# Self attention on one core: slots taken two at a time, all jobs at full tile shape, projections as three products of rounded parts, GpSimd splitting the maxima

## What is computed

```python
def _L1_ffn_ref(x, Wq, Wkv, Ws, Wo, bo):
    s = jax.nn.sigmoid(x @ Ws)
    vals, idx = jax.lax.top_k(s, TOPK)
    scores = jnp.zeros_like(s).at[bi, ti, idx].set(vals)
    q = (x @ Wq).reshape(b, t, H, DH).transpose(0, 2, 1, 3)
    kv = (x @ Wkv).reshape(b, t, 2, H, DH).transpose(2, 0, 3, 1, 4)
    k, v = (kv[0], kv[1])
    attn = jax.nn.softmax(jnp.einsum('bhid,bhjd->bhij', q * scale, k), axis=-1)
    out = jnp.einsum('bhij,bhjd->bhid', attn, v)
    proj = jnp.einsum('bhtd,hde->bhte', out, Wo) + bo[None, :, None, :]
    return jnp.einsum('bhte,bth->bte', proj, scores)
```

## Time and profile before

| | |
|---|---|
| time, median of 3 runs | 2458.72 us (2457.88 to 2459.5) |
| the profiled execution's own time | 2457.71 us |
| its span, first to last instruction | 2455.7 us |
| PE, share of the span | 85% |
| DVE, ACT, POOL | 60%, 37%, 36% |
| TensorE's granted clock, mean | 0.923 of full speed |
| `self_gates`, first to last instruction | about 1487 to 1559 us |
| `self_attention`, until PE's loop starts | about 1559 to 1625 us |
| one batch of the loop (four units) | 100.05 us |

### The profile page before, as it was taken

How to read it: one execution, slowest core, us unless ns; L and a number is a source line. 1 busy time by engine, 2 the same in 40 slices (tenths; PEclk the granted TensorE clock), 3 DMA queues, 4 the chain that set the end, 5 groups by cost and what they waited for, 6 DMA issues and landing times. The chain is left out here.

```text
span 2455.7 us, 38024 instructions
## 1 busy us (share of the span) xinstructions
PE 2085.7 (85%) x11977; PEld 1378.2 (56%) x11977; DVE 1471.1 (60%) x2334; ACT 918.0 (37%) x1568; POOL 884.1 (36%) x801
## 2 busy tenths in 40 slices
PE   5760499999999972799999997389999999999997
PEld 2660499999999970333333337145555455555454
DVE  7840244554555443799998875356575666656655
ACT  4520133333333420366666662122232332323332
POOL 0057723551555013455453330113333333333322
PEclk9955799999999985799999995699999999999998
DMA  6572233323332234244443333233232322323231
GB/s 226 203 295 103 79 119 125 113 79 130 118 120 68 78 96 123 77 127 131 126 125 113 111 108 131 58 83 74 61 91 65 86 61 61 94 63 84 65 77 49
DMA packets 155315, 257.46 MB, mean 105 GB/s; under 512 B 25414, under 2 KB 74606, under 8 KB 151914
## 3 DMA queue, kind: packets, MB, share of 16 engines
q1 hardware_dynamic: 111778, 176.24, 25.0%
q0 software_dynamic: 15328, 44.61, 5.5%
q10 hardware_dynamic: 28160, 35.99, 4.5%
HBM read 124.81 MB, written 75.43 MB: 82 GB/s over the span
## 5 line engine op out<-in xcount | busy, mean ns | idle before, releaser
L1207 DVE TENSOR_REDUCE ca_negmax<-ca_na 128x2 f32<-128x1024 f32 x272 | 330.8, 1220 | 42.1 <-PE ca_na L935 39.7
L1057 ACT ACTIVATE ca_pr<-ca_st 128x512 f32<-128x512 f32 x512 | 279.3, 599 | 131.8 <-PE ca_st L949 130.2
L680 DVE TENSOR_TENSOR ex_h<-ex_up,ex_sg 128x512 f32<-128x512 f32 x136 | 94.0, 692 | 306.0 <-ACT ex_sg L643 198.7
L1839 DVE TENSOR_REDUCE sa_negmax<-sa_na 128x1 f32<-128x512 f32 x272 | 182.7, 674 | 132.5 <-PE sa_na L1659 127.9
L935 PE MATMUL ca_na<-ca_k_stack,ca_q_stack 64*128 64x512 f32 x544 | 212.0, 467 | 23.8 <-DVE ca_negmax L1207 21.0
L603 PE MATMUL ex_gp<-ex_xp,moe_gu_p 128*128 128x256 f32 x1632 | 222.2, 286 | 1.6 <-DVE ex_xp L666 1.4
L949 PE MATMUL ca_st<-ca_q_stack,ca_k_stack 64*128 64x512 f32 x512 | 205.7, 462 | 18.0 <-ACT ca_pr L1057 17.4
L616 PE MATMUL ex_yp<-moe_dn_p,ex_hp 128*128 128x256 f32 x1632 | 209.3, 286 | 11.9 <-DVE ex_hp L670 11.9
L603 PE MATMUL ex_up<-ex_xp,moe_gu_p 128*128 128x256 f32 x1632 | 218.1, 283 | 0.0
L1827 POOL TENSOR_TENSOR sa_acc<-sa_acc,sa_pr 128x1024 f32<-128x1024 f32 x64 | 151.6, 2368 | 170.2 <-ACT sa_pr L1778 170.2
L1823 POOL TENSOR_TENSOR sa_acc<-sa_pr 128x1024 f32<-128x1024 f32 x32 | 75.2, 2349 | 381.6 <-ACT sa_pr L1778 381.6
(11 more groups left out here) (284 smaller groups left out, 3786.4 us busy)
## 6 DMA issues: line engine op xcount, KB each, us to landing
sa_q<-sa_qh SPq DMA_DIRECT2D x140, 128.0 KB
sa_k<-sa_kh SPq DMA_DIRECT2D x140, 128.0 KB
ex_raw_m<-masks ACTq DMA_DIRECT2D x34, 512.0 KB, 3.7
moe_gu_raw<-gateupT POOLq DMA_DIRECT2D x8, 2048.0 KB, 8.3
ca_k_stack<-cross_k SPq DMA_DIRECT2D x216, 64.0 KB
ca_q_stack<-cross_q SPq DMA_DIRECT2D x216, 64.0 KB
expert_rows<-rt_zeros SPq DMA_DIRECT2D x20, 512.0 KB, 15.4
cross_q<-ca_qp SPq DMA_DIRECT2D x10, 1024.0 KB, 5.1
```

The costliest lines, as they stand in the source:

```text
L1057: act.activation(pr[:, s // HG % 2, s % HG, :], st[s % 2][:, :], ACT.Exp, scale=DK ** -0.5).then_inc(exp_done, 1)
L1207: dve.tensor_reduce(negmax[:, g % 2, 1 - r % 2, :, r // 2], na[r % 2][:, :, :], AX.X, ALU.max, negate=True).then_inc(max_done, 1)
L1839: dve.tensor_reduce(negmax[:, par, h, t:t + 1], na[s % 2][:, :], AX.X, ALU.max, negate=True).then_inc(max_done, 1)
```

## The change

The changed kernel computes the same. It differs in these points.

- The loop over 8 slots becomes a loop over 4 rounds of two slots. A round is: both `score_b`, a place for jobs, both `score_a`, a place for jobs, `values`, a place for jobs. So there are 12 places for jobs in a unit.
- q, k and v are computed from rounded parts: x and the weights are split in `self_gates` (ACT copies the rounded part, POOL subtracts), and each product is the three terms of the list `TERMS`, so 6 rounded matmuls for q and 6 for k. v is made for two pairs of heads and two token tiles at a time (12 rounded matmuls of 256 columns), in units 0 (two), 2 and 3 (one each). x goes through HBM in both parts, 1 MB for a batch instead of 512 KB.
- The maxima are split by POOL instead of DVE, at the start of the unit that uses them. The stationary side is a full 128 columns, mostly zero, and the product is rounded.
- Gates and bias are matmuls over all 128 partitions (the unused ones are zero), with the bias in three terms too.

```diff
 def self_gates(nc, io, x, mv, rstd, ident, iota8, xT_d, gT_d, weights, wo, bo3):
+            def low(b):
+                pool.wait_ge(xh_ready, b + 1)
+                pool.tensor_tensor(xp[:, b % 2, 1, :, :], xt[:, :, b * S:(b + 1) * S], xp[:, b % 2, 0, :, :].bitcast(F32), ALU.subtract).then_inc(xl_ready, 1)
+            for b in range(2):
+                low(b)
+            for i, n in enumerate(weights):
+                pool.wait_ge(wh_ready, i + 1)
+                pool.tensor_tensor(weights[n][:, 1, :, :], raw[n][:, :, :], weights[n][:, 0, :, :].bitcast(F32), ALU.subtract).then_inc(wl_ready, 1)
+                low(b + 1 + i)
...
-                sp.wait_ge(xt_ready, (b + 1) * TB)
-                sp.dma_start(xT_d.rearrange("(c p) n -> p c n", p=P)[:, :, b * S:(b + 1) * S], xt[:, :, b * S:(b + 1) * S]).then_inc(stored, 16)
+                sp.wait_ge(xl_ready, b + 1)
+                sp.dma_start(xT_d.rearrange("(r c p) n -> p r c n", r=2, p=P)[:, :, :, b * S:(b + 1) * S], xp[:, b % 2, :, :, :].bitcast(F32)).then_inc(x_put[b % 2], 16)
...
             def copy_out(t):
+                if t % TB == TB - 1:
+                    b = t // TB
+                    act.wait_ge(xt_ready, t + 1)
+                    if b >= 2:
+                        act.wait_ge(x_put[b % 2], 16 * (b // 2))
+                    act.copy(xp[:, b % 2, 0, :, :], xt[:, :, b * S:(b + 1) * S]).then_inc(xh_ready, 1)
+                    if b == 1:
+                        act.wait_ge(w_in, 16 * 5)
+                        for n in weights:
+                            act.copy(weights[n][:, 0, :, :], raw[n][:, :, :]).then_inc(wh_ready, 1)
 def self_attention
+        sel2 = m.sb("sel2", [P, SH * H], F32R)
+        gparts = m.sb("gparts", [P, S], F32R)
+        xT = m.sb("xT", [P, 2, KC, S], F32R)
+        parts = m.sb("parts", [P, 2, 2, TB, P], F32R)
...
+            JOBS += {0: [("q", 0, 0), ("k", 0, 2), ("v2a", 0, 4), ("sum", 0, 5), ("v2b", 0, 6), ("m0", 0, 7), ("m1", 0, 9), ("gate", 0, 10)],
+                     1: [("q", 1, 0), ("k", 1, 2), ("o0", 1, 4), ("sum", 1, 5), ("o1", 1, 6), ("m0", 1, 7), ("m1", 1, 9), ("gate", 1, 10)],
+                     2: [("q", 2, 0), ("k", 2, 2), ("v0a", 2, 4), ("sum", 2, 5), ("m0", 2, 6), ("m1", 2, 7), ("gate", 2, 9)],
+                     3: [("q", 3, 0), ("k", 3, 2), ("v0b", 3, 4), ("sum", 3, 5), ("m0", 3, 6), ("m1", 3, 7), ("gate", 3, 9)]}[g]
+        FIRST = ["q", "k"] * 3 + ["v0a", "v0b", "m0", "m1"]
+        TERMS = ((0, 0), (0, 1), (1, 0))
...
-                        sp.wait_ge(misc_full, job(b, g, "v") + 1)
+                        sp.wait_ge(misc_full, job(b, g, "v2b") + 1)
                         load_x(after)
...
+                    for i in range(KC):
+                        for wr, xr in TERMS:
+                            last = pe.matmul(misc[:, :], w[:, wr, i, c * P:(c + 1) * P], xT[:, xr, i, :],
+                                             start=(i == 0 and (wr, xr) == TERMS[0]), stop=(i == KC - 1 and (wr, xr) == TERMS[-1]))
...
+                    for r in range(TB):
+                        for s in (2 * r, 2 * r + 1):
+                            score_b(g, s, u)
+                        jobs(g, 3 * r, b)
+                        for s in (2 * r, 2 * r + 1):
+                            score_a((g + 2) % C, b if g < 2 else b + 1, s, u + 2)
+                        jobs(g, 3 * r + 1, b)
+                        if r == 0:
...
+                            values((g - 1) % C, TB - 1)
...
+                            values(g, t)
+                        jobs(g, 3 * r + 2, b)
...
+            pool.memset(parts[:, :, :, :, :].bitcast(F32), 0.0).then_inc(set_up, 1)
+            def split_max(a, par, h):
+                pool.wait_ge(max_done, a * SLOTS + (h * TB + TB + 2))
+                pool.tensor_tensor(parts[:, par, h, :, H], negmax[:, par, h, :], ones[:, 0:TB], ALU.mult).then_inc(mh_ready, 1)
+                pool.wait_ge(mh_ready, a * 2 + (h + 1))
+                pool.tensor_tensor(parts[:, par, h, :, H + 1], negmax[:, par, h, :], parts[:, par, h, :, H].bitcast(F32), ALU.subtract).then_inc(ml_ready, 1)
...
                 for g in range(C):
                     u = b * C + g
+                    for h in range(2):
+                        split_max(u + 1, (g + 1) % 2, h)
                     pool.wait_ge(misc_full, job(b, g, "sum") + 1)
...
+                if h == 0 and t == 0 and not (isinstance(a, int) and a < 2):
+                    dve.wait_ge(ml_ready, a * 2 - 2)
...
-                if t == TB - 1:
-                    dve.wait_ge(max_done, a * SLOTS + (s + 3))
-                    dve.tensor_copy(parts[:, par, h, :, 0].bitcast(F32R), negmax[:, par, h, :]).then_inc(mh_ready, 1)
-                    dve.wait_ge(mh_ready, a * 2 + (h + 1))
-                    dve.tensor_tensor(parts[:, par, h, :, 1].bitcast(F32R), negmax[:, par, h, :], parts[:, par, h, :, 0], ALU.subtract).then_inc(ml_ready, 1)
```

More of the change, by code:

```diff
@@ L1611, in project @@
                     if name == "q":
                         pe.wait_ge(xT_in, b * 16 + 16)
-                if name == "v":
-                    for t in range(piece * TB // count, (piece + 1) * TB // count):
-                        for i in range(KC):
-                            last = pe.matmul(misc[:, t * P:(t + 1) * P], xT[:, i, t * P:(t + 1) * P], wv[:, i, c * P:(c + 1) * P],
-                                             start=(i == 0), stop=(i == KC - 1))
-                else:
-                    w = wq if name == "q" else wk
-                    for i in range(piece * KC // count, (piece + 1) * KC // count):
-                        last = pe.matmul(misc[:, :], w[:, i, c * P:(c + 1) * P], xT[:, i, :], start=(i == 0), stop=(i == KC - 1))
@@ L1622, in project @@
-                if piece == count - 1:
-                    last.then_inc(misc_full, 1)
+                    w = weights["sWq" if name == "q" else "sWk"]
+                    for i in range(KC):
+                        for wr, xr in TERMS:
+                            last = pe.matmul(misc[:, :], w[:, wr, i, c * P:(c + 1) * P], xT[:, xr, i, :],
+                                             start=(i == 0 and (wr, xr) == TERMS[0]), stop=(i == KC - 1 and (wr, xr) == TERMS[-1]))
+                last.then_inc(misc_full, 1)
@@ L1690, in _, with jobs @@
                         max_rows(nf - 2 + h, 0, 0, h)
+            def jobs(g, p, b):
+                u = b * C + g
+                for name in jobs_at(g, p):
+                    n = job(b, g, name)
+                    if name[0] == "m":
+                        max_rows(n, u + 1, (g + 1) % 2, int(name[1]))
+                    elif name == "sum":
+                        sums(n, u)
+                    elif name == "gate":
+                        if g == 1:
+                            pe.wait_ge(gT_in, b * 32 + 32)
+                        gates(n, (g - 1) % C)
+                    elif name[0] == "o":
+                        output(n, b, int(name[1]))
+                    else:
+                        project(n, name, (g + 3) % C, b if g == 0 else b + 1)
             with pe.Fori(0, B) as b:
@@ L1727, in _ @@
             for i in range(2):
-                output(last_job(f"o{i}"), B, i, (0, 1))
+                output(last_job(f"o{i}"), B, i)
         @block.scalar
@@ L1768, in _, with jobs @@
             act.activation(tock[:, :], ident[:, 0:1], ACT.Exp)
+            def jobs(g, p, b):
+                for name in jobs_at(g, p):
+                    n = job(b, g, name)
+                    if name == "sum":
+                        sum_out(n, b * C + g)
+                    elif name in "qk":
+                        head(n, name, None, (stack_in[(g + 2) % C], b * LOAD + (2 * LOAD if g >= 2 else LOAD)))
+                    elif name[0] == "v":
+                        v_out(n, name)
+                    elif name[0] == "m":
+                        m_out(n, (g + 1) % C, int(name[1]))
             with act.Fori(0, B) as b:
@@ L1891, in _, with jobs @@
                     maximum(a, s, a)
+            def jobs(g, p, b):
+                u = b * C + g
+                for name in jobs_at(g, p):
+                    n = job(b, g, name)
+                    if name in "qk":
+                        rest(n, name, u * 2 + (6 + "qk".index(name)))
+                    elif name == "gate":
+                        gate(n, u)
+                    elif name[0] == "o":
+                        add(n, int(name[1]), (b + (B - 1)) % B)
             with dve.Fori(0, B) as b:
```

200 lines of the change are left out of this document (91 added, 109 removed).

## The result

The changed kernel takes 2332.89 us, median of 4 runs (2331.47 to 2333.42), where the kernel before takes 2458.3 (2455.19 to 2459.5, 4 runs). The ratio is 0.9491, 95% interval 0.9474 to 0.9507, so 125 us went. The forecast was 2334. Its profiled execution took 2333.27 us, its span is 2331.0.

The account below looks back on a forecast made before the run. The prediction took PE to bound the loop, busy 96.1 of a batch's 100.05 us. It saved 16.6 us a batch, 133 in eight, and added 8 in `self_gates`: -125, so 2334 us (2316 to 2350).

Parts of the forecast that it names:

- E: Rival: gaps on PE drop the loop's clock to 1.2 GHz for part of each batch, slower than before; 2%.
- q, k and v: Loop, PE: rounded matmuls save 2.4 us a batch for q and k, 1.8 for v.
- Maxima: Loop, PE: a maxima job falls from 1.14 to 0.48 us, saving 5.3 us a batch over eight jobs.
- A: Rival: rounded 128-column matmuls cost 0.235 us, so maxima save 1.6 instead of 5.3; total 2363 us; 14%.
- Gate: Loop, PE: at full depth each of four gates saves 0.385 us, 1.5 a batch.
- Bias: Loop, PE: the bias falls from 0.845 to 0.12 us, four jobs saving 2.9 us a batch.
- Sums: Loop, PE: sums right behind `values` in the same tile shape save 4 x 0.35 = 1.4 us a batch.
- Old and new waits: Loop, PE, per batch: 4.0 us of waits go; 1.9 come behind ACT's exponential, 0.8 from missed handovers.
- `self_gates` +8: Block before the loop: ACT copies +3.5, last copy +1, POOL memset +1.8, POOL holding DVE +2; in all +8 us.
- C: Rival: POOL's 11 subtractions hold DVE fully in `self_gates`, +24 us on the +2 taken; total 2358; 8%.
- Start and end of `self_attention`: Outside the loop's batches: changes of a few us both ways, taken as 0, bounds -3 and +3.
- D: Rival: neither the wait behind the exponential nor missed handovers come, -2.7 us a batch; total 2313; 5%.

Follow-up runs that it names:

- experiment 7: Changed kernel with scores and jobs ordered slot by slot, plus the old fp32 two-column maxima matmul: 2348.38 us; or plus short gate and bias matmuls: 2331.57 us.
- experiment 4: Changed kernel with job m1 at place 8, behind `values`, in all units: 2317.09 us.
- experiment 8: Changed kernel with ACT's copies and POOL's subtractions of the weights moved behind the sigmoid in `self_gates`: 2332.57 us.
- experiment 10: Changed kernel without POOL's subtractions of x, its low part set to zero once: 2336.08 us, a single run.
- experiment 6: Changed kernel with the maxima split by DVE again and POOL's four operations gone: 2339.31 us.
- experiment 9: Changed kernel with the slot-by-slot order and the weights' copies and subtractions behind the sigmoid: 2307.72 us.

## Why the prediction was right, and where its steps were not

- **What bounds the loop.** Right. PE's work and its waits fill a batch before and after, at a clock of 1.00, so E never came near. Eight batches gave 126.5 of the 124.7 us.
- **q, k and v.** Right in sum: 4.2 forecast, 4.1 when undone. q and k were worth more (2.9 for 2.4) and v less (1.2 for 1.8). The 1.885 us of v before start right behind `values` and hold part of what leaving their tile shape costs, which the 1.205 of `values` had counted already (after the change k takes 1.49 behind `values`, q 1.37 behind scores).
- **Maxima.** Right to a tenth in size: 5.3 forecast, 4.8 measured with no wait about (experiment 7). The forecast priced all eight jobs like m0, which stands between scores. m1 stood right behind `values` in the kernel before:

```profile
1919.94 0.39 PE L1659 MATMUL sa_na<-sa_k,sa_q 128*128 128x512 f32 x1
1920.26 1.08 PE L1675 MATMUL sa_av<-sa_pr,sa_vw 128*64 128x512 f32 x4
1921.27 1.03 PE L1604 MATMUL sa_misc<-all_ident,sa_parts 128*2 128x128 f32 x8
...
1922.57 0.40 PE L1668 MATMUL sa_st<-sa_q,sa_k 128*128 128x512 f32 x1
```

  `values` and m1 together take 1922.57 - 1919.94 less two paces, 2.16, where 1.205 + 1.14 would be 2.345, so m1 cost 0.96 and not 1.14, 0.74 less in a batch. The reason given failed too: "the eight records are short and the rest is entering and leaving a tile two columns wide". Between scores the fp32 product costs 0.80 - 0.39 = 0.41 of it and the two columns 0.25; before `values`, which change the tile shape themselves, the columns cost nothing. The bound from 256 columns held: four rounded matmuls of 128 columns take 0.39 to 0.44 us, so A fell. The Trainium skill's figure ("TensorE: Matmul & The Clock Gate", section "Back-to-back issue gap"), 81 ns for each, would have made 0.32; the trace has about 0.11, for this rounded type.
- **Gate.** Right: 0.385 forecast, 0.38 measured between scores. Where the gate stands before `values` now, in units 0 and 1, undoing it costs 0.17 or, behind a wait, nothing.
- **Bias.** Half an output job takes 1.84 us where it took 2.55, 0.71 saved for 0.725 forecast. I laid it to "the bias and its 8-row tile"; the depth is 0.29 of it, the rest fp32.
- **Sums.** Right: `values` and sums take 2.06 together, counted as before, against twice 1.205: 0.35 saved in a unit, as forecast. No run undoes this term alone.
- **Old and new waits.** The 4.0 went, the new one is 0.4 to 0.5 us in each unit for the reason given (experiment 4 removes it by a place). Of the 0.8 for near misses, two of about 0.23 us are there in unit 1, each right behind an output job (`values` to sums is 1.13 us between starts there, 0.91 in the unit shown). I take them for waits for DVE's addition of the output; the trace lists none so short.
- **The sum of the loop failed by 0.8 us a batch**: 16.6 forecast, 15.8 seen, 6 us in all. The terms one by one give 4.1 for q, k and v, 4.8 for the maxima, 1.5 for gates, 2.8 for biases and 1.4 for sums, 14.6 where 15.3 was forecast. So most of the miss is in the work. The largest step in it is m1 behind `values`: the change of tile shape between them was counted twice, 0.74 in a batch. Smaller errors go both ways. With 4.0 of old waits and 2.4 of new ones the terms make 16.2. The last 0.4 is argued, not isolated by a run: the list counts a wait from the end of the record before it, so it leaves out a part. Ahead of m1, PE lost 2216.54 - 2215.64 - 0.235 = 0.67 us where 0.50 is listed.
- **`self_gates` +8**: measured +6.2 to the first memset of `self_attention`, and 1.8 for the memset that was added there. The sum was right by luck in part. ACT's copies of the weights cost 2.8 for 3.5, the sigmoid came 1.0 later as forecast, and the hold of DVE by POOL cost 3.3 where I took 2 and C had 26. Another 1.6 stands in no listed wait. Against that the end of the block became 2.5 shorter, from DVE's last `sg_gl` to the memset (6.7 for 9.3): SP stores the gates there in two parts instead of three, and issuing the third took 1.79 before. The forecast had no term for it, and no run isolates it. C's mechanism is real (experiments 8 and 10), but DVE's lead hides most of each hold. PE felt it with the subtractions of x and of the weights together, and felt neither alone: without those of the weights amid the tiles no wait is left (experiment 8, which moved ACT's copies as well), nor without those of x (experiment 10). The largest waits, 1.02 and 1.06, come in the stretch where POOL did four subtractions without a pause and, as I read it, DVE's lead of up to four tiles ran out.
- **Start and end of `self_attention`**: 0 with bounds of 3 either way. The end became 4.2 shorter, outside the bound.
- **D** holds as a mechanism, by another kernel: 2313 for a loop without new waits, 2314.17 in the order of single slots.

Against the forecast span of 2330.7 the errors are loop +6.5, the two blocks ahead of it -0.5, end -4.2 and an earlier start of `self_gates` -1.4: they cancel to 0.4 us (0.3 by the spans). So a total right to 1 us is luck; what was right is the path and the size of its terms. The -1.4 isn't a term of the change either: the layer ahead ended 3.1 sooner because the clock stayed high there, and 1.7 later for another reason (last section). Experiments 6 and 8 show layers outside the change moving by up to 5 us between kernels, so a forecast of the total can't be judged finer than that here.

## What to carry to other kernels

Once PE is busy all the time, a wait and the work around it are one account: a longer job may cost less than its own time because it stands in the time of a wait, and a shorter one brings less until the order is changed. So test a term with the waits gone, and read what stands ahead of a shared bank's copy on its engine before the jobs are placed. Split an operation's price into its number format, its width or depth and its neighbours before you give one of them the credit, price a job at each place where it stands, and put large POOL operations where DVE's queue has a lead or nothing waits for it.

## What was not expected of the hardware

- A change of tile shape is paid once, whichever neighbour asks for it: the two-column matmul cost 0.25 us more than the full one before scores and nothing before `values`, which are 64 columns wide. `values` share it on both sides: behind them m1 cost 0.96 for 1.14 (kernel before), and before them the short gate costs 0.17 for 0.38 (experiment 7).
- The unchanged layers ahead of `self_gates` ended at different times: DVE's first operation of the block starts 1485.4 us after the span's start in one kernel (short gate and bias with single slots, experiment 7) and at 1490.9 in another (experiment 8), both on one chip. The four runs of experiment 8 agree within 4 us, so it is hardly chance from run to run. The traces show more than half of it. The last two output jobs of the cross attention, eight matmuls each, took 1.99 us each in the changed kernel and 3.78 in experiment 8:

```profile
1479.06 1.99 PE L884 MATMUL ca_misc<-cross_wo,ca_outT 128*128 128x256 f32 x8 [0.68 <-ACT ca_outT L1033]
```

```profile
1481.28 3.78 PE L884 MATMUL ca_misc<-cross_wo,ca_outT 128*128 128x256 f32 x8 [0.68 <-ACT ca_outT L1033]
```

  The granted clock was 1.00 from 1470 to 1480 and 0.95 from there to 1488 in the changed kernel, and 0.81 and 0.50 in experiment 8 (1.00 is 2.4 GHz, 0.50 is 1.2). From this job to DVE's first operation of `self_gates` it is 6.6 us at the high clock and 9.65 at the low one: 3.1 of the 5.3 us between these two. The kernel before and experiment 6 have the low clock there too (3.78), which makes experiment 6 late by 2.8; experiments 7 and 9 have the high one. Why the clock falls earlier in some kernels stays open: PE was busy 6.1 of the 10 us from 1470 in the changed kernel, and 6.8 in experiment 8. The other 2.2 us stay open as well; no run was made for either.
- DVE was busy 7 us more a batch with the split of the maxima back, where before it was 20.8 more than after. The cast and the subtraction show it, in one batch of the kernel before and of experiment 6 (busy us, mean ns):

```profile
L1844 DVE TENSOR_TENSOR sa_parts<-sa_negmax,sa_parts 128x4 fp32r<-128x4 f32 x9 | 12.1, 1345 | 0.3
L1842 DVE CAST sa_parts<-sa_negmax 128x4 fp32r<-128x4 f32 x8 | 10.7, 1340 | 0.3
```

```profile
L1901 DVE CAST sa_parts<-sa_negmax 128x4 fp32r<-128x4 f32 x9 | 7.9, 874 | 0.3
...
L1903 DVE TENSOR_TENSOR sa_parts<-sa_negmax,sa_parts 128x4 fp32r<-128x4 f32 x8 | 1.3, 167 | 0.3
```

  The cast takes 170 ns alone. Most of the difference is the subtraction, 1345 ns in the kernel before and 167 in experiment 6. How much of POOL's additions such an operation meets depends on the order around it, so relieving DVE was worth less time on DVE than before showed, and nothing on PE.
